# Softmax stages of a graph network kernel: logits and values in PSUM, one tensor laid out features outside

## The reference

```python
# L1
h = node_h @ W_fc.T
eh = edge_h @ W_fcr.T
alpha = _segment_softmax(eh, dst, N)
agg = segment_sum(alpha * (h[src] + eh), dst)
# L3: d comes from the edge attributes by two small dense layers
w1 = features @ W1; w2 = features @ W2; w3 = features @ W3
logits = w1[target] - w2[source] + d
a = softmax of logits over the edges of one target
out = segment_sum(a * (w3[source] + d), target)
```

## Time and profile before

| | us |
|---|---|
| median of 3 runs | 19512.13 |
| lowest and highest | 19508.68, 19513.66 |
| the profiled execution | 19526.0 |
| its span in the trace | 19524.3 |
| DVE busy in the span | 10891.7 (56%) |
| POOL busy in the span | 14542.5 (74%) |
| ACT busy in the span | 2935.3 (15%) |
| PE busy in the span | 3963.0 (20%) |

### The profile page before, as it was taken

The page is one execution under the profiler, slowest core; times in us unless marked ns, Lnnn a source line. Parts: engine busy times, 40 slices in busy tenths (PEclk is TensorE's granted clock), DMA queues, the critical chain, the costliest instruction groups (busy, mean ns, idle before and its releaser), DMA issues. The chain is left out here.

```text
span 19524.3 us, 114146 instructions
## 1 busy us (share of the span) xinstructions
PE 3963.0 (20%) x22754; PEld 3029.3 (16%) x22754; DVE 10891.7 (56%) x30752; ACT 2935.3 (15%) x3836; POOL 14542.5 (74%) x14151
## 2 busy tenths in 40 slices
PE   2323276662111121111111122222110000100000
PEld 2222165562000010000000011111110000000000
DVE  6777575562333323332333357777745555598887
ACT  1111122121111111111111112222200000011111
POOL 5777677777777777776777768888767777677775
PEclk6555598886555555555555555555555555555555
DMA  2222200001222222221222223333222222243343
GB/s 90 59 59 59 63 30 29 26 30 38 59 59 59 57 54 59 59 59 52 59 59 59 61 71 105 105 103 100 97 63 79 79 79 78 81 135 134 133 136 102
DMA packets 595626, 1425.33 MB, mean 73 GB/s; under 512 B 323513, under 2 KB 324046, under 8 KB 546867
## 3 DMA queue, kind: packets, MB, share of 16 engines
q1 hardware_dynamic: 141422, 929.39, 12.4%
q0 software_dynamic: 452336, 477.62, 11.9%
q10 hardware_dynamic: 1348, 12.78, 0.2%
HBM read 670.38 MB, written 754.41 MB: 73 GB/s over the span
## 5 line engine op out<-in xcount | busy, mean ns | idle before, releaser
L791 POOL DMA_INDIRECT rows<-tab,idx x11648 | 12001.8, 1030 | 3643.5 <-issue 3547.7
L1081 DVE TENSOR_TENSOR_SCAN rows<-held,last,rows 128x64 f32<-128x64 f32 (+1 forms) x6656 | 1619.9, 325 | 3947.4 <-DMA rows<-tab,idx 3947.4
L483 POOL DMA_INDIRECT rec<-recs,sidx x1664 | 1720.6, 1034 | 547.7 <-issue 507.2
L860 PE MATMUL dist_ps<-dist_w,a3T 65*128 65x512 f32 x416 | 392.7, 1099 | 4858.2 <-ACT a3T L884 3760.6
L1276 DVE TENSOR_TENSOR_SCAN H<-logits,H,neg_d 128x52 f32<-128x52 f32 x4096 | 903.1, 301 | 42.4 <-ACT logits L1226 30.9
L1301 DVE TENSOR_TENSOR_SCAN DN<-XB,last,PB 128x52 f32<-128x52 f32 x4096 | 909.4, 301 | 5.8
L1301 DVE TENSOR_TENSOR_SCAN DN<-XB,last,VB 128x52 f32<-128x52 f32 x4096 | 911.4, 300 | 0.0
L860 PEld LDWEIGHTS dist_ps<-dist_w,a3T 65*128 65x128 f32 x416 | 122.0, 324 | 5001.0 <-issue 4743.0
L920 DVE TENSOR_REDUCE held<-SQ 128x16 f32<-128x1024 f32 x208 | 254.7, 1225 | 765.7 <-ACT SQ L891 765.7
L1234 ACT ACTIVATE PB<-XB 128x3328 f32<-128x3328 f32 x64 | 190.5, 2977 | 3255.9 <-DVE XB L1281 3255.9
L905 ACT ACTIVATE held<-held 128x16 f32<-128x16 f32 x104 | 17.5, 168 | 4160.5 <-DVEq L922 4160.5
(11 more groups left out here) (361 smaller groups left out, 15506.5 us busy)
## 6 DMA issues: line engine op xcount, KB each, us to landing
sums<-rows SPq DMA_DIRECT2D x104, 2048.0 KB, 6.8
sums<-DN SPq DMA_DIRECT2D x64, 3328.0 KB
rows<-tab,idx POOLq DMA_INDIRECT x11648
maxes<-H SPq DMA_DIRECT2D x64, 1664.0 KB
spread<-zeros SPq DMA_DIRECT2D x26, 2080.0 KB
own<-spread SPq DMA_DIRECT2D x26, 2080.0 KB, 7.4
dists<-Y SPq DMA_DIRECT2D x104, 512.0 KB
side<-in_attr SPq DMA_DIRECT2D x32, 1664.0 KB
```

The source lines that it names most:

```text
L483: pool.indirect_dma_start(rec, bass.IndirectOffsetOnAxis(ap=idx[b][:, j:j + 1], axis=0), recs[b][:, j, :], None).then_inc(moved[b], 16)
L791: pool.indirect_dma_start(rows[b][:, j, :], None, table, bass.IndirectOffsetOnAxis(ap=idx[b][:, j:j + 1], axis=0)).then_inc(rows_in[b], 16)
L860: t = pe.matmul(self.p1[:, 8 * h:8 * h + 8, :].rearrange("p a f -> p (a f)"), self.a3T[:, :], dist_w[:, h * 512:(h + 1) * 512], start=True ...
L1081: dve.tensor_tensor_scan(rows[b][:, :, f], k, rows[b][:, :, f], last[:, f:f + 1], ALU.mult, ALU.add).then_inc(scanned, 1)
```

## The change

It touches `softmax_pass` and, in two lines, the setup.

- `XB`, `PB` and `VB` are now edges outside, [P, TS, F], as the logits and rows are. A new tile `XF`, [P, F, TS], holds the second exponential (the fade) features outside; ACT writes it so, in two halves of 32 features with a count on `faded` each (L1240). In L3 `XF` is the memory of `keep_d` and `keep_s`, no longer needed there, which is why these two become one tile `keeps`.
- The logits of both stages are in PSUM, `lg_p`, seven of the eight banks. In L1, PE multiplies straight into it, and ACT's copy L1226 with the tile `L1b` is gone. One bank is left for `pt`, so that PE transposes group g + 1 after ACT has copied group g. PE's first product of a chunk waits for `ml2` of the chunk before (L1295), the last reader of the logits.
- The values are formed in place, in PSUM: logits = rows + logits (L1291), in both stages. For L3 that needs other rows: `q3` becomes W2 + W3 in the setup (a 128x128 add on DVE), since d + w3 = (d - w2) + (w2 + w3).
- L1295 is VB = logits * PB. The last scans go half by half: 32 of `PB` and 32 of `VB` after the fade's first half, the rest after the second.
- In L3 SP loads the next `side` after `ml` (L1273), no longer after `valued`.

```diff
-            L1b = alloc(c, "logits", [P, TS, F]) if one else ps(c, "logits", [P, TS, F])
+            lg_p = ps(c, "logits", [P, TS, F])
-            XB, PB = alloc(c, "XB", [P, F, TS]), alloc(c, "PB", [P, F, TS])
-            VB = alloc(c, "VB", [P, F, TS])
-            by_edge = lambda t: t[:, :, :].rearrange("p f t -> p t f")
+            XB, PB, VB = (alloc(c, n, [P, TS, F]) for n in ("XB", "PB", "VB"))
+            if one:
+                XF = alloc(c, "XF", [P, F, TS])[:, :, :]
+            else:
+                XF = keeps[:, :, :].rearrange("p a n -> p (a n)").rearrange("p (f t) -> p f t", f=F)
...
+                    turn(i, b, 0)
                     for g, (h0, n) in enumerate(GR):
...
+                        pe.wait_ge(ts, ch * NGR + g + 1)
+                        if g + 1 < NGR:
+                            turn(i, b, g + 1)
+                        if g == 0 and not start:
+                            pe.wait_ge(ml2, ch)
                         for h in range(n):
...
+                            o = lg_p[:, 2 * (h0 + h):2 * (h0 + h) + 2, :].rearrange("p a f -> p (a f)")
+                            t = pe.matmul(o, aT_[(b * NGR + g) % 2][:, h, :], bd["fcr"][:, :], start=True, stop=True)
...
-                    act.activation(XB[:, :, :], XB[:, :, :], ACT.Relu).then_inc(t1, 1)
-                    act.wait_ge(t1, ch * 2 + 2)
-                    act.activation(XB[:, :, :], XB[:, :, :], ACT.Exp, scale=-1.0).then_inc(faded, 1)
+                    for h in range(2):
+                        x = XB[:, :, h * HF:(h + 1) * HF]
+                        act.activation(x, x, ACT.Relu).then_inc(t1, 1)
+                        act.wait_ge(t1, ch * 3 + 2 + h)
+                        act.activation(XF[:, h * HF:(h + 1) * HF, :].rearrange("p f t -> p t f"), x,
+                                       ACT.Exp, scale=-1.0).then_inc(faded, 1)
...
-                    dve.tensor_tensor(by_edge(XB), l, Hh[:, 0:TS, :], ALU.subtract).then_inc(dk, 1)
+                        dve.wait_ge(faded, ch * 3)
+                    dve.tensor_tensor(XB[:, :, :], l, Hh[:, 0:TS, :], ALU.subtract).then_inc(dk, 1)
...
-                        dve.tensor_tensor(by_edge(VB), v, l, ALU.add).then_inc(valued, 1)
-                    else:
-                        dve.tensor_tensor(by_edge(VB), v, side[:, :, :], ALU.add).then_inc(valued, 1)
+                    dve.wait_ge(maxed, ch + 1)
+                    dve.tensor_tensor(l, v, l, ALU.add).then_inc(valued, 1)
...
-                    dve.tensor_tensor(VB[:, :, :], VB[:, :, :], PB[:, :, :], ALU.mult).then_inc(ml2, 1)
-                    dve.wait_ge(faded, ch * 2 + 2)
+                    dve.tensor_tensor(VB[:, :, :], l, PB[:, :, :], ALU.mult).then_inc(ml2, 1)
...
-                    for s_, a in enumerate((PB, VB)):
-                        for f in range(F):
-                            dve.tensor_tensor_scan(DN[:, :, s_ * F + f], XB[:, f, :], a[:, f, :],
-                                                   last[:, s_ * F + f:s_ * F + f + 1], ALU.mult, ALU.add).then_inc(summed, 1)
+                    for h in range(2):
+                        dve.wait_ge(faded, ch * 3 + 2 + h)
+                        for s_, a in enumerate((PB, VB)):
+                            for f in range(h * HF, (h + 1) * HF):
+                                dve.tensor_tensor_scan(DN[:, :, s_ * F + f], XF[:, f, :], a[:, :, f],
+                                                       last[:, s_ * F + f:s_ * F + f + 1], ALU.mult, ALU.add).then_inc(summed, 1)
```

More of the change, by code:

```diff
@@ L98, in gnn_resnorm @@
     ident = alloc(top, "ident", [P, P])
-    keep = {o: alloc(top, f"keep_{o}", [P, NT]) for o in "ds"}
+    keeps = alloc(top, "keeps", [P, 2, NT])
+    keep = {o: keeps[:, n, :] for n, o in enumerate("ds")}
     neg = alloc(top, "neg_d", [P, NT])
@@ L177, in _ @@
                     dve.tensor_copy(bd[n][:, :], tp[:, :]).then_inc(tr_done, 1)
+                link(dve.tensor_tensor(bd["q3"][:, :], bd["q3"][:, :], bd["q2"][:, :], ALU.add))
                 link(dve.reduce_sum(mean[:, :], bd["d2"][:, :], axis=AX.X))
@@ L1127, in softmax_pass @@
                 aT_ = [alloc(c, f"attrT{n}", [P, 4, P]) for n in range(2)]
[L1128 to L1132, removed]
+                pt = ps(c, "pt", [P, 4, P])
             def val_of(b):
@@ L1191, in _, with turn @@
             def _(pe):
+                def turn(i, b, g):
+                    h0, n = GR[g]
+                    for h in range(n):
+                        r = side[:, 2 * (h0 + h):2 * (h0 + h) + 2, :].rearrange("p a f -> p (a f)")
+                        t = pe.transpose(pt[:, h, :], r, ident[:, :])
+                    t.then_inc(tr, 1)
                 def step(i, b):
                     ch = i * 2 + b
+                    start = isinstance(i, int) and i == 0 and b == 0
                     pe.wait_ge(side_in, ch * 16 + 16)
+                    turn(i, b, 0)
                     for g, (h0, n) in enumerate(GR):
[L1196 to L1199, removed]
-                        for h in range(n):
[L1201 to L1208, removed]
+                        pe.wait_ge(ts, ch * NGR + g + 1)
[3 more added lines that the diff above has]
+                            pe.wait_ge(ml2, ch)
+                        for h in range(n):
+                            o = lg_p[:, 2 * (h0 + h):2 * (h0 + h) + 2, :].rearrange("p a f -> p (a f)")
+                            t = pe.matmul(o, aT_[(b * NGR + g) % 2][:, h, :], bd["fcr"][:, :], start=True, stop=True)
                         t.then_inc(lg, 1)
@@ L1214, in _, with turned @@
             def _(act):
-                def logits(i, b):
+                def turned(i, b):
                     ch = i * 2 + b
@@ L1221, in logits @@
                             act.wait_ge(lg, ch * NGR + g - 1)
[L1222 to L1227, removed]
+                        act.activation(aT_[z][:, 0:n, :], pt[:, 0:n, :], ACT.Copy).then_inc(ts, 1)
                 def fades(i, b):
@@ L1234, in fades @@
                     act.activation(PB[:, :, :], XB[:, :, :], ACT.Relu, scale=-1.0).then_inc(t1, 1)
[L1235 removed]
+                    act.wait_ge(t1, ch * 3 + 1)
                     act.activation(PB[:, :, :], PB[:, :, :], ACT.Exp, scale=-1.0).then_inc(faded, 1)
[L1237 to L1239 removed]
+                    for h in range(2):
[4 more added lines that the diff above has]
+                                       ACT.Exp, scale=-1.0).then_inc(faded, 1)
                 if one:
[L1241 removed]
+                    turned(0, 0)
                     fades(0, 0)
[L1243 removed]
+                    turned(0, 1)
                     fades(0, 1)
                     with act.Fori(1, NC // 2) as i:
[L1246 removed]
+                        turned(i, 0)
                         fades(i, 0)
[L1248 removed]
+                        turned(i, 1)
                         fades(i, 1)
@@ L1266, in step @@
                     if one:
[L1267 removed]
+                        dve.wait_ge(lg, (ch + 1) * NGR)
                     else:
```

19 lines of the change are left out of this document (7 added, 12 removed).

## The result

The changed kernel takes 20247 us, median of 4 runs (20243.22 to 20253.75); the kernel before beside it 19510 us. The ratio is 1.0379, 95% interval 1.0361 to 1.0397: 3.8% slower, where 4.2% faster was forecast.

What follows compares the result with a forecast made beforehand. POOL's gathers were taken to bound L1 and L3, with DVE setting their pace. Savings of 554 us in L1 and 258 in L3, together 812, took 19512 to 18700 us, 4.2% faster; range 18650 to 18870.

Steps and rivals of the forecast that it cites:

- What bounds the kernel: L1 and L3: POOL's gathers are the bound; large DVE operations with both inputs in SBUF stop POOL.
- POOL's pace: Gathers per chunk: L1 loses all four long ones, 82.6 to 65.1 us; L3 keeps one costing 3.2 us, 76.4 to 68.3.
- DVE fast enough: DVE's own work falls to 59.7 us a chunk in L1, 63.4 in L3, so it still waits about 5 us for rows.
- The scans: Last scans reading PB and VB across, step 64 values: no cost taken, upper bound 6.9 us a chunk.
- ACT: Relu and Exp with crosswise halves: 1.6 to 3.1 us a half, both ready before DVE wants them.
- The logits of L1: PE's products wait for ml2; at most 3.6 us a group, done by R + 32.8, wanted at R + 38.0: no cost.
- The PSUM sum: Rival: L1291, summing in PSUM, still stops POOL, 2.7 us in 62 chunks, 167 us: 18867 us; chance 0.07.
- Strided reads make DVE the bound: Rival: the last scans pay 6.9 us a chunk on DVE, 112 us in all: 18812 us; chance 0.07.
- The slower rival: ACT's crosswise Exp very slow; at 16 us a half, 154 us more, 19666 us; chance 0.02.

Runs made afterwards that it cites:

- the repaired version: Changed kernel with PB and VB features outside again, written across in halves by ACT and DVE, last scans reading in order: 18700.7 us beside 19509 us.

## Why the prediction was wrong

- *What bounds the kernel.* Right: POOL, and how often DVE stops it. The rule drawn from it, that large operations with both inputs in SBUF stop POOL, held for every one of them. But the kernel before has 128 scans a chunk with both inputs in SBUF, which don't, and the prediction did not ask why. That question leads to the miss. (Why scans in order don't stop POOL, while L1293, a large operation in order, stretched a gather to 3.63 us, no run here tells.)
- *POOL's pace.* The four stops went, the one under L1273 cost 2.3 us and not 3.2. Right.
- *DVE fast enough.* Large operations took 3.62 to 3.63 us and DVE waited for rows. Right, but by 27 to 32 us and not 5, since POOL stood still under the scans.
- *The scans.* **This is the step that failed.** "I take no cost" weighed DVE's time alone, and there it was right, 7.1 us for 32, 28.4 for all, as before. What the crosswise second input does to POOL was no term of the sum. The chunks took 25.1 us more than forecast in L1 and 24.7 in L3; 31 times both is 1544 us, of the 1547 between 18700 and 20247. The row it leaned on, L1276, reads its first input across and its second, `neg`, in order, and that is harmless, as the run with the first input across shows. The scans of the sum passes (L1081) read rows across as second input, but their first, `held`, is in PSUM, and so it is in L2. No row of the kernel before had both inputs in SBUF with the second across, so both ends of the bound should have been left open for POOL as well.
- *ACT.* A crosswise half took 3.64 us, above the 1.6 to 3.1 given; hidden all the same, DVE waited 4.8 us for it in all of L3.
- *The logits of L1.* Right; from one copy of ACT to the next 1.35 us in the steady part, well under the 3.6 allowed:

```profile
12052.65 3.63 ACT L1240 ACTIVATE XF<-XB 128x1664 f32<-128x1664 f32 x1
...
12091.14 0.60 ACT L1226 ACTIVATE attrT<-pt 128x512 f32<-128x512 f32 x1 [1.90 <-PE pt L1196]
12092.49 0.60 ACT L1226 ACTIVATE attrT<-pt 128x512 f32<-128x512 f32 x1 [0.75 <-PE pt L1196]
```

- *The rivals.* The PSUM sum doesn't stop POOL: 0.94 us beneath it. "Strided reads make DVE the bound" had the right operations and the wrong engine: its price was put on DVE. The slower rival was put on ACT. The range, with 0.02 on slower, was too sure of a list of costs that had been made for one engine at a time.

The other terms of the sum are borne out by the repaired version, 18700.7 us in one execution; the forecast change with nothing but its scans in order was never timed beside 19510 us.

## What to carry to other kernels

Where POOL issues gathers, cost each edit of a DVE operation twice: what it does to DVE, and what it does to POOL. Keep the second input of a train of scans with both inputs in SBUF in order, at most 8 bytes from value to value; or put one input in PSUM; or, as far as the traces show it, let DVE finish every fourth (its worth in time was not measured where POOL is the bound). When a rule read from a trace ("both inputs in SBUF stop POOL") has an exception in the same trace, find out what makes the exception before an edit touches it.

## What the runs showed of the hardware

- The step of the second SBUF input of a scan decides whether POOL's gathers run beside it: 4 and 8 bytes yes, 16 and 256 bytes no (as a rule one gather of 26.5 to 28 us for 128 scans). 8 bytes were tried only in the slower surroundings and 16 only in the quicker, 4 and 256 in both. Why the second input and not the first is open. The first input's step doesn't matter, nor does a second input in PSUM.
- DVE itself is no slower for it, 222 ns from scan to scan either way, so only POOL's rows show the cost.
- ACT writing with a step of 208 bytes takes 3.64 us for 1664 values, 2.3 times the 1.59 of the earlier trace rows.
- The same programs ran in two kinds of surroundings, 19510 and 25550 us for the kernel before, and one chip was met in both. In the slower kind DVE stands idle 0.4 to 1.8 us before many short instructions while gathers run, for nothing that the profile shows. Why is open: the gathers' own times are the same (median 945 and 944 ns). There the order of the two kernels is reversed, because DVE and not POOL is the bound, so a result for kernels of this kind holds for the surroundings it was measured in.
